# Attention scores as one full float32 product a head, in place of three products of rounded parts

## The reference

```python
x = x + xattn(layernorm(x), ctx)   # x: 4096 x 512, ctx: 3202 x 512
x = x + ffn(layernorm(x))          # 8 experts, the best 2 of each token
# xattn: 16 heads of 32
q = (queries @ Wq + bq).reshape(B, L, 16, 32)
k = (keys @ Wk + bk).reshape(B, S, 16, 32)
v = (values @ Wv + bv).reshape(B, S, 16, 32)
A = softmax(einsum('blhe,bshe->bhls', q, k) / sqrt(32))
out = einsum('bhls,bshd->blhd', A, v) -> (B, L, 512) @ Wo + bo
```

## Time and profile before

| | |
|---|---|
| median of 3 runs | 2391.94 us (2391.36 to 2395.5) |
| profiled execution | 2391.14 us; span from first to last instruction 2389.3 us |
| TensorE busy | 2279.1 us, 95% of the span; mean granted clock 0.979 of full speed |
| VectorE busy | 2017.9 us, 84% |
| ScalarE busy | 1856.0 us, 78% |
| projections | about 0 to 280 us |
| attention | about 293 to 1935 us |
| output projection and experts | the rest |

### The profile page before, as it was taken

How to read it: one execution, slowest core, us unless ns; L and a number is a source line. 1 busy time by engine, 2 the same in 40 slices (tenths; PEclk the granted TensorE clock), 3 DMA queues, 4 the chain that set the end, 5 groups by cost and what they waited for, 6 DMA issues and landing times. The chain is left out here.

```text
span 2389.3 us, 49150 instructions
## 1 busy us (share of the span) xinstructions
PE 2279.1 (95%) x19632; PEld 1098.8 (46%) x19632; DVE 2017.9 (84%) x1866; ACT 1856.0 (78%) x2155; POOL 506.4 (21%) x631
## 2 busy tenths in 40 slices
PE   8999689999999999999999999999999999789898
PEld 7878523333333333333333333333333357578786
DVE  4358479999999999999999999999999998866555
ACT  3223279999999999999999999999999966534332
POOL 2213211311111111111111111111111112145664
PEclk9999889999999999999999999999999999889999
DMA  7436595434465434446445444644444368634463
GB/s 266 169 133 211 177 282 116 103 94 105 114 170 122 107 90 113 113 114 178 102 101 115 113 101 126 154 112 112 108 98 108 94 177 269 208 103 143 142 201 123
DMA packets 140700, 333.70 MB, mean 140 GB/s; under 512 B 28694, under 2 KB 61430, under 8 KB 123324
## 3 DMA queue, kind: packets, MB, share of 16 engines
q0 software_dynamic: 43008, 193.75, 33.3%
q1 hardware_dynamic: 95132, 129.20, 16.5%
q10 hardware_dynamic: 2336, 7.60, 0.9%
HBM read 131.16 MB, written 82.78 MB: 90 GB/s over the span
## 5 line engine op out<-in xcount | busy, mean ns | idle before, releaser
L1125 ACT ACTIVATE probs<-psum 128x1536 f32<-128x1536 f32 x800 | 1165.1, 1456 | 0.0
L1290 PE MATMUL psum<-probs,v_st 128*32 128x512 f32 x6400 | 854.9, 606 | 0.2 <-ACT probs L1125 0.2
L1243 PE MATMUL psum<-q_st,k_st 32*128 32x512 f32 x9600 | 780.6, 426 | 49.3 <-ACT probs L1122 32.1
L1243 PEld LDWEIGHTS psum<-q_st,k_st 32*128 32x128 f32 x9600 | 402.8, 184 | 753.1 <-ACT probs L1122 435.5
L1199 DVE TENSOR_TENSOR even_sums<-even_sums,probs 128x2048 f32<-128x2048 f32 x288 | 658.6, 2287 | 81.1 <-ACT probs L1125 80.1
L1199 DVE TENSOR_TENSOR odd_sums<-odd_sums,probs 128x2048 f32<-128x2048 f32 x256 | 588.2, 2298 | 6.1 <-ACT probs L1125 6.0
L1122 ACT ACTIVATE probs<-psum 128x512 f32<-128x512 f32 x800 | 481.1, 601 | 48.2 <-PE psum L1243 34.2
L1290 PEld LDWEIGHTS psum<-probs,v_st 128*32 128x32 f32 x6400 | 126.1, 108 | 290.0 <-issue 279.1
L2075 PE MATMUL psum<-we_hi,wo 128*128 x624 | 219.3, 413 | 8.3 <-issue 5.0
L949 POOL DMA_DIRECT2D pile<-probs x96 | 85.2, 888 | 489.9 <-DMA pile<-probs 268.9
L2075 PEld LDWEIGHTS psum<-we_hi,wo 128*128 128x128 f32 x624 | 119.7, 192 | 35.4 <-issue 9.6
(11 more groups left out here) (229 smaller groups left out, 2261.4 us busy)
## 6 DMA issues: line engine op xcount, KB each, us to landing
pile<-probs POOLq DMA_DIRECT2D x128, 1024.0 KB, 7.4
token_rows<-rows SPq DMA_DIRECT2D x8, 1028.0 KB, 6.6
xn<-in_x SPq DMA_DIRECT2D x16, 512.0 KB, 6.5
qh_scratch<-o_hi SPq DMA_DIRECT2D x8, 1024.0 KB, 4.5
ql_scratch<-o_lo SPq DMA_DIRECT2D x8, 1024.0 KB, 7.5
q_st<-qh_scratch SPq DMA_DIRECT2D x32, 256.0 KB, 3.8
q_st<-ql_scratch SPq DMA_DIRECT2D x32, 256.0 KB, 4.8
token_rows<-in_x SPq DMA_DIRECT2D x1, 8192.0 KB, 43.5
```

The costliest lines, as they stand in the source:

```text
L1125: act.activation(probs[:, p, 1:HG, :], psum[:, bank(t, 1):bank(t, 1) + HG - 1, :], ACT.Exp, bias=-WIDEST, scale=SCALE).then_inc(exp_done, 1)
L1243: return nc.tensor.matmul(psum[:, bank(t, h), :], k_st[rows, part, t * P:(t + 1) * P], q_st[it % 2][rows, of, :], start=start, stop=stop)
L1290: mm = nc.tensor.matmul(psum[h * DH:(h + 1) * DH, bank, :], lhs(h), rhs(h), start=start, stop=stop)
```

## The change

Keys and queries are no longer split for attention. ScalarE writes the whole value once (`o_sb`, float32), VectorE's `k_low` and `q_low` are gone (28 and 32 instructions), and waits on them become waits on ScalarE's result. One scratch tensor each (`k_scratch`, `q_scratch`) takes the place of two, with half the stores and loads. `squares` reads the whole value. In attention a score tile is four float32 matmuls, one a head, in place of twelve float32r ones, and the step for the last keys is one in place of three. The weighing of values, the exponentials, the sums and all that follows are as they were.

```diff
-TERMS = ((0, 0), (0, 1), (1, 0))
...
-                    sp.wait_ge(k_hi, (c + 1) * NG)
-                    sp.wait_ge(k_lo, (c + 1) * NG)
-                    sp.dma_start(kh_d[:, :, ds(c * CH, w)], o_hi[b][:, :, 0:w].bitcast(F32)).then_inc(k_stored[b], 16)
-                    sp.dma_start(kl_d[:, :, ds(c * CH, w)], o_lo[b][:, :, 0:w].bitcast(F32)).then_inc(k_stored[b], 16)
+                    sp.wait_ge(k_out, (c + 1) * NG)
+                    sp.dma_start(k_d[:, :, ds(c * CH, w)], o_sb[b][:, :, 0:w]).then_inc(k_stored[b], 16)
...
-                def q_low(c, b, js):
-                    for j in js:
-                        dve.wait_ge(q_hi, c * NG + (j + 1))
-                        dve.scalar_tensor_tensor(out=o_lo[b][:, j, :], in0=psum[:, 4 + j, :], scalar=bq_col[:, j:j + 1],
-                                                 in1=o_hi[b][:, j, :].bitcast(F32), op0=ALU.add, op1=ALU.subtract).then_inc(q_lo, 1)
-
...
-        k_st = sb("k_st", [P, 2, S], F32R)
+        k_st = sb("k_st", [P, S], F32)
...
-            for part, src in enumerate((kh_d, kl_d)):
-                sp.dma_start(k_st[:, part:part + 1, first:first + n].bitcast(F32), src[:, ds(j, 1), first:first + n]).then_inc(count, 16)
+            sp.dma_start(k_st[:, first:first + n], k_d[:, ds(j, 1), first:first + n].rearrange("p o s -> p (o s)")).then_inc(count, 16)
...
-                    for term in range(len(TERMS)):
-                        last = term == len(TERMS) - 1 and not shifted
-                        for h in range(HG):
-                            mm = products(it, t, h, term, term == 0, last)
+                    for h in range(HG):
+                        rows = slice(h * DH, (h + 1) * DH)
+                        mm = nc.tensor.matmul(psum[:, bank(t, h), :], k_st[rows, t * P:(t + 1) * P], queries_of(it, 0)[rows, :], start=True, stop=not shifted)
...
-                    for term, (part, of) in enumerate(TERMS):
-                        mm = nc.tensor.matmul(psum[0:REST_ROWS, REST_BANK, :], rest_k[:, j, part, 0:REST_ROWS], q_st[b][:, of, :],
-                                              start=term == 0, stop=term == len(TERMS) - 1 and not shifted)
+                    mm = nc.tensor.matmul(psum[0:REST_ROWS, REST_BANK, :], rest_k[:, it // NC, 0:REST_ROWS], queries_of(it, 0), start=True, stop=not shifted)
```

More of the change, by code:

```diff
@@ L141, in projections @@
     L, D, S, KT, NG, NC, NSC, NT, LAST, TPC = (g[n] for n in "L D S KT NG NC NSC NT LAST TPC".split())
-    x, ctxT, kh_d, kl_d, v_d, qh_d, ql_d, SCALE = (g[n] for n in "x ctxT kh_d kl_d v_d qh_d ql_d SCALE".split())
+    x, ctxT, k_d, v_d, q_d, SCALE = (g[n] for n in "x ctxT k_d v_d q_d SCALE".split())
     last_w = S - (NSC - 1) * CH
@@ L158, in projections @@
         a_lo = [sb(f"a_lo{b}", [P, KT, CH], F32R) for b in range(2)]
-        o_hi = [sb(f"o_hi{b}", [P, NG, CH], F32R) for b in range(2)]
-        o_lo = [sb(f"o_lo{b}", [P, NG, CH], F32R) for b in range(2)]
+        o_sb = [sb(f"o_sb{b}", [P, NG, CH], F32) for b in range(2)]
         v_sb = [sb(f"v_sb{b}", [P, TPC, D], F32) for b in range(2)]
@@ L194, in projections @@
         v_mm = sem("v_mm")
-        k_hi = sem("k_hi")
-        k_lo = sem("k_lo")
+        k_out = sem("k_out")
         v_out = sem("v_out")
@@ L304, in store_q @@
                 def store_q(c, b):
[L305 to L308, removed]
+                    sp.wait_ge(q_out, (c + 1) * NG)
+                    sp.dma_start(q_d[:, :, ds(c * CH, CH)], o_sb[b][:]).then_inc(q_stored[b], 16)
                 def next_x(c, b):
@@ L451, in ctx_low @@
                                       ALU.subtract).then_inc(c_lo, 1)
[L453 to L458, removed]
                 def v_chunk(c, b, i, w):
@@ L555, in q_chunk @@
                 def q_chunk(c, b, i):
-                    q_low(c, b, range(half))
                     if not (isinstance(c, int) and c == 0):
@@ L562, in q_chunk @@
                         ln(c + 2, b, i + 1)
-                    q_low(c, b, range(half, NG))
                 q_chunks(dve, q_chunk)
@@ L718, in load_queries @@
 def load_queries(sp, g, b, it, count):
-    for part, src in enumerate((g["qh_d"], g["ql_d"])):
-        sp.dma_start(g["q_st"][b][:, part, :].bitcast(F32), src.rearrange("p j l -> p (j l)")[:, ds(it * CH, CH)]).then_inc(count, 16)
+    sp.dma_start(g["q_st"][b][:, 0, :].bitcast(F32), g["q_d"].rearrange("p j l -> p (j l)")[:, ds(it * CH, CH)]).then_inc(count, 16)
 def load_shift(sp, g, b, it, count):
@@ L802, in attention @@
     S, SP_, NG, NC, NT, LAST, SCALE, D = (g[n] for n in "S SP_ NG NC NT LAST SCALE D".split())
-    kh_d, kl_d, v_d, qh_d, ql_d, shift_d = (g[n] for n in "kh_d kl_d v_d qh_d ql_d shift_d".split())
+    k_d, v_d, shift_d = (g[n] for n in "k_d v_d shift_d".split())
     NIT = NG * NC
@@ L921, in queries_in @@
         def queries_in(it, shifted):
-            per = 48 if shifted else 32
+            per = 32 if shifted else 16
             return per * (it // 2 + 1) - (16 if shifted and it % 2 == 0 else 0)
@@ L1015, in weighted @@
                         if n == 0:
-                            for part, src in enumerate((kh_d, kl_d)):
-                                sp.dma_start(rest_k_raw[:, :, part, :], src[:, :, S - LAST:S]).then_inc(rest_k_in, 16)
+                            sp.dma_start(rest_k_raw[:], k_d[:, :, S - LAST:S]).then_inc(rest_k_in, 16)
                         if n == WO_AFTER:
@@ L1237, in _, with queries_of @@
             def _(pe):
-                def products(it, t, h, term, start, stop):
-                    part, of = TERMS[term]
-                    rows = slice(h * DH, (h + 1) * DH)
-                    return nc.tensor.matmul(psum[:, bank(t, h), :], k_st[rows, part, t * P:(t + 1) * P], q_st[it % 2][rows, of, :], start=start, stop=stop)
+                def queries_of(it, part):
+                    return q_st[it % 2][:, part, :].bitcast(F32)
                 def scores(it, t, shifted):
@@ L1264, in scores @@
                             row = slice(h * DH, h * DH + 1)
-                            mm = nc.tensor.matmul(psum[:, bank(t, h), :], shift_ones[row, :], q_st[it % 2][row, SHIFT_PART, :], start=False, stop=True)
+                            mm = nc.tensor.matmul(psum[:, bank(t, h), :], shift_ones[row, :], queries_of(it, SHIFT_PART)[row, :], start=False, stop=True)
                     mm.then_inc(s_ready, 1)
                 def rest_scores(it, shifted):
-                    b, j = it % 2, it // NC
                     pe.wait_ge(exp_done, it * STEPS + REST_TILE - 1)
@@ L1273, in rest_scores @@
                         pe.wait_ge(rest_k_built, HG)
-                    for term, (part, of) in enumerate(TERMS):
-                        mm = nc.tensor.matmul(psum[0:REST_ROWS, REST_BANK, :], rest_k[:, j, part, 0:REST_ROWS], q_st[b][:, of, :],
-                                              start=term == 0, stop=term == len(TERMS) - 1 and not shifted)
+                    mm = nc.tensor.matmul(psum[0:REST_ROWS, REST_BANK, :], rest_k[:, it // NC, 0:REST_ROWS], queries_of(it, 0), start=True, stop=not shifted)
                     if shifted:
-                        mm = nc.tensor.matmul(psum[0:REST_ROWS, REST_BANK, :], rest_shift[:, 0:REST_ROWS], q_st[b][:, SHIFT_PART, :], start=False, stop=True)
+                        mm = nc.tensor.matmul(psum[0:REST_ROWS, REST_BANK, :], rest_shift[:, 0:REST_ROWS], queries_of(it, SHIFT_PART), start=False, stop=True)
                     mm.then_inc(s_ready, 1)
@@ L1355, in _ @@
                                             w = min(CH, S - b * CH)
-                                            for term, (part, of) in enumerate(TERMS):
-                                                mm = pe.matmul(psum[:, b, 0:w], q_st[0][rows, of, t * P:(t + 1) * P],
-                                                               k_st[rows, part, b * CH:b * CH + w], start=term == 0, stop=term == len(TERMS) - 1)
+                                            mm = pe.matmul(psum[:, b, 0:w], queries_of(0, 0)[rows, t * P:(t + 1) * P],
+                                                           k_st[rows, b * CH:b * CH + w], start=True, stop=True)
                                         mm.then_inc(ma_mm, 1)
-                    pe.wait_ge(ma_q_in, (NIT * 2 + 3) * 16)
+                    pe.wait_ge(ma_q_in, (NIT + 2) * 16)
                     for it in range(NIT):
```

102 lines of the change are left out of this document (48 added, 54 removed).

## The result

The changed kernel takes 2512.18 us (median of 4 runs, 2511.0 to 2513.17) against 2391.84 us before (median of 4 as well): 1.0497 times as long, 95% interval 1.0481 to 1.0513, so 5% slower. The prediction was 2523 us, in a range of 2500 to 2600.

A forecast was written before the change was run, and what follows sets the result against it. The prediction took TensorE to set attention's pace, at 1.89 us a tile. From 2391.14 us, 143.7 for slower rounds less 11.4 given back made 2523 us, 5.5% slower, in a range of 2500 to 2600.

The forecast's parts named there:

- What bounds the kernel: Attention's steady state: TensorE sets the pace at 1.89 us a tile; ScalarE needs 1.80, so has 0.09 to spare.
- The float32 tile: Attention's scores: load 0.10, two waves of 0.43, drain 0.11; 1.07, rounded 1.08 us, 0.18 more than 0.90.
- The high end: Score tile: the second wave's weight load is not hidden, giving 1.17 us a tile, 0.27 more; total 2593 us.
- A round: Attention round: 25 x 0.18 + 0.17 (last keys) - 0.18 (shorter starting wait) = 4.49 us longer; 143.7 over 32 rounds.
- What was given back: Savings from removed splitting work, stores and loads at the projections and attention's first round: 11.4 us in sum.
- The store: End of the projections: without the low part's second store the next block starts about 3.9 us earlier.
- The second tile's wait of 2.48: Start of attention: the second score tile's wait for the keys' low part shrinks by up to 2.5 us.
- the piled tiles: First round, ScalarE's waits of 7.46 and 2.83 us: slower tiles ahead and halved key traffic together save 4 us.
- A short float32 wave by row groups: Rival, score tile: a wave takes 0.23 us, the tile 0.67, ScalarE sets the pace; total 2319 us; 7 in 100.
- waves that don't lie side by side: Rival, scores: heads' float32 products stagger into five waves, 2.36 us a tile, about 3550 us, or eight, 4600; 8 in 100.
- ScalarE did not hide a part: Denies the rival that 1.89 is ScalarE's own pace, leaving 0.09 a tile, so 2452 us; 5 in 100.
- The path without shift: Rival: bound on scores from whole keys triggers the shifted path, hundreds of us more; with all else 2 in 100.

The follow-up runs named there:

- storing twice: The changed kernel with every chunk of keys and queries stored a second time, into scratch tensors that nothing reads: 2514.72 us.
- the product alone: The kernel before with one float32 matmul a head on the high parts; low parts still made, stored and loaded: 2517.93 us.
- the data path alone: The changed kernel with three float32r products a head of the same undivided keys and queries in place of the float32 one: 2380.79 us.

## Why the prediction was right

**What bounds the kernel.** That TensorE set the pace and ScalarE had 0.09 us to spare was shown from both sides: more passes made every tile longer by what they take (2.07 and 2.13 us a tile), and with one pass the tiles came 1.80 apart, as read from the earlier trace rows.

**The float32 tile.** Taken from the values' waves by column groups, it was to be 1.07 to 1.08 us. It is 1.07. This is the sum of the terms forecast: a load of 0.10, two waves of 0.43, a drain of 0.11. The high end, a second load that shows, did not come: the loads are over before the second wave starts, and the first gap is 0.54. A tile grew by 0.17, where the sum took 0.18.

**A round.** 4.49 was predicted and 4.23 measured. 25 tiles at 0.17 are 4.3, the last keys' step 0.19 (0.17 predicted), and the wait at a round's start shrank by 0.17 (0.18 predicted). These make 4.3, which is what separates the usual rounds (50.6 and 54.88). The mean round of the kernel before (50.66) also holds small delays, and so 4.23 is left. Over 32 rounds the term was 8 us too large (143.7 for 135.4), nearly all of it from the gaps read to 0.01 us and taken at the upper digit: 0.01 on a tile is 8 us.

**What was given back.** 11.4 us were predicted. 32 x 4.23 is 14.4 more than the 121.0 that the profiled span grew by, so 3 more came back. By place:

- Up to attention's first large exponential 3.9 + 1 = 4.9 were predicted, and it starts at 288.62 in place of 294.78, 6.2 earlier. The store was right in place and size: the two block starts, 284.38 and 278.53, are 5.85 apart, of which TensorE's earlier end of the projections is 1.9 (its last matmul there starts at 276.62 and not 278.54), so 3.9 is the store; storing twice gave 2.7 of that back as a wait. Of the 1.9, 1.0 is ScalarE's earlier start on the queries (160.33 in place of 161.37), as predicted; the other 0.9 comes in steps of 0.15 with the later chunks of queries, which the prediction had at nothing. 0.3 lie between the block's start and the exponential.
- The second tile's wait of 2.48 comes behind that exponential, so it belongs to the first round. There 4.5 longer, less 2.5 and less 4, made 2.0 shorter, and 1.9 was measured. The number is right and the reason is half luck. The wait of 2.48 went (it is 1.5 with the product alone). But the product alone already shortens this round by 1.7, and the lighter data path adds only 0.2 with the float32 product in place. A tile that waits for a transfer anyway is not made longer by a slower product, as I read it: the longest gap between two large exponentials in this round is 9.4 us before and 7.5 with the product alone. The prediction had this for the piled tiles (0.7 + 1.6) and put the rest down to the lighter traffic. Against it stand the first tiles, which run at half clock: a record group of 2.09 where it was 1.65.
- Rounds 2 and 32, each counted from its first large exponential, grow by 3.9, a little less than the mean. In the stage after attention, which the diff does not touch, 1.3 came back, and I have no cause for it.

The account of the span closes: -6.2 - 1.9 + 3.9 + 29 x 4.23 + 3.9 - 1.3 = 121. The forecast was 11 us too high because the rounds' term was 8 too large and what was given back 3 too small. The 11.4 are near the 11.0 of the data path alone, but those were measured with three short products; with the float32 product the data path gives 5.8 (2517.93 less 2512.18), and the rest of the 14.4 comes with the product itself, most of it in the first round.

**The rivals.** A short float32 wave by row groups, and waves that don't lie side by side, are both excluded by the two waves 0.53 apart. ScalarE did not hide a part: it follows the scores by 0.14. The path without shift was taken. The first rival's sum can be checked all the same: two short products without the lighter data path are its case, 2391 - 61 = 2330 us, and measured were 2328.19. What it left out is that VectorE is at 99% beside ScalarE there.

## What to carry to other kernels

Count a float32 matmul as four passes of a float32r one, whether heads are laid side by side by rows or by columns; a split into three rounded products is a pass cheaper, and every pass left out counts in full as long as TensorE sets the pace. Fewer instructions and half the stores and loads look like less work, but here they gave back 11 us with three short products and 6 with the float32 one, against 126, because most of the removed work lay under TensorE's. Before paying for precision ask how much of it is wanted: one float32r product of undivided keys and queries takes 2308.6 us, 3.5% less than the kernel before (and two products 2.7% less), and at that point ScalarE sets the pace with VectorE as full, so that the second pass left out buys little. Moving work from VectorE to a chain of transfers that is nearly full itself made the kernel 136 us slower.

## What the runs showed of the hardware

All of this is at a granted clock of 1.00. A float32r wave keeps the array for 0.23 us (952.27 to 952.50). A float32 wave takes 0.43, worked out from a tile of 1.07 less the 0.21 that is not waves in a tile of 0.90 with three short ones; it is a little less than two float32r waves: four float32r products took 1.14 us a tile, a float32 product 1.07. Weights of the second half of a float32 product load while the first wave runs, in row groups (all eight loads within 0.31 us of the start, the second wave 0.54 behind it) as in column groups (0.16 us, and 0.46). By the gaps, only the first load of a group (0.10 us for 128 columns, 0.03 for 32) and 0.11 us of drain at each change between the groupings show. For the scores and values of one tile that is an estimated 0.35 us of 2.07 in which no columns stream.
